# Cross-attention and a quantised FFN on one core: queries of batches 2 to 7 turned in 32-row blocks by SP and VectorE, mask terms and weight widening on ScalarE, and TensorE products that nobody reads

## The chip, the cores and the metric

One core of one Trainium2 chip runs the whole program in one launch. The metric is the device time of that launch in microseconds, the median of several runs. TensorE, VectorE (DVE), ScalarE (ACT), GpSimd (POOL) and SyncE (SP, which here only issues DMAs) run side by side and meet through semaphores. P = 128 is the number of partitions.

## What is computed

Eight batches of 512 rows of 512 numbers, cut to what matters:

```python
def xattn(v, k, q, mask, W, b):            # v = k = context, q = layernorm(x)
    scores = einsum('bqd,bkd->bqk', q, k) / sqrt(512)
    scores = where(mask, -1e9, scores)
    atted = einsum('bqk,bkd->bqd', softmax(scores), v)
    return einsum('bdl,ol->bdo', swapaxes(atted, -1, -2), W) + b
x = x + xattn(context, context, layernorm(x), mask, W_merge, b_merge)
y = fake_quant_activation(layernorm(x))    # one scale for the whole tensor, int8 grid
h = fake_quant_activation(silu(y @ q(w_gate).T) * (y @ q(w_up).T))
x = x + h @ q(w_down).T                    # q: each weight row on its own int8 grid; I = 1408
```

## The kernel before

**Two parts.** `attention()` does the first line for all batches and, beside it, brings the FFN weights on their grids; `ffn()` does the rest. Both write their five engine programs by hand: each engine executes its list in order, and every wait is a `wait_ge` on a semaphore. The order of the work is thus the order of the code of each engine.

**Precision.** In attention every float32 matrix is split in two float32r halves, `_hi` (a rounded copy, ScalarE) and `_lo` (the rest, VectorE or GpSimd), and a product is the sum hi x hi, hi x lo, lo x hi (`product`, lines 805 to 817): 12 matmuls of 128x512 for each 128-row tile, 48 for each of the three products of a batch. These are, on TensorE: `scores(n, k)` for tile k of batch n (lines 819 to 826), `merged(m, k)` for the batch before (m = n - 1, lines 828 to 833), and `mixed(n, k)` (lines 835 to 840), the product of probabilities and merge matrix. The loop is at lines 856 to 880. All three use the four PSUM banks `mm[k]`, so `scores(n + 1, k)` waits (`g_ready`) until `mixed_hi` (ScalarE, line 440) and `mixed_lo` (VectorE, line 632) have taken `mm[k]` of batch n, `merged` waits until the mask step has read the scores (`masked`), and `mixed` until the residual has been added (`x1_made`).

**The queries.** `norm1` (ScalarE, line 451) writes the normalised rows `qn`. TensorE turns them, `transposes(n + 1, T + k)` (line 789) ahead of `mixed(n, k)`: four 128x128 transposes into bank `tr[k]`. `transposed_hi` (ScalarE) and `transposed_lo` (VectorE, line 527) take them out as `qT_hi` and `qT_lo`.

**The context.** Its transposed form already avoids TensorE from batch 1 on: `load_cb` (SP, line 238) loads 32-row blocks of the context to the partitions where a transpose would put the block, in pieces of 32 numbers, and `turn_c` (VectorE, line 572) turns each 32x32 block in place. `turned_hi` (ScalarE) and `turned_lo` (GpSimd, line 377) split it.

**The rest of a batch.** VectorE: `mask_and_max` (line 583) adds the mask term `mneg`, takes the row maximum and, in a second step, `nmax`, its negative scaled; `invert_sum`, `probs_lo`; `row_stats1`; `row_bias1`; then for batch n - 1 `add_residual`, `row_stats2`, `row_min2`; then `weights_scale` (line 637), the largest of each row of a few weight tiles. ScalarE: `exps`, `probs_hi`, `norm1`, `context_hi`, `mixed_hi` and `weights_round` (line 467), which writes int8 `w8`. VectorE widens `w8` to float16 (`weights16`, line 666) at the start of the next batch, and SP turns it with DMA transposes (`turn_w`, line 262). GpSimd: `add_bias`, the powers of -1/2 (`make_rstd1`, `make_rstd2`), `make_mneg` (line 340, a whole batch in one step of 2,048 columns), `turned_lo`, `make_c_lo` (line 373). SP's order in a batch is at lines 299 to 322.

**Between the parts** each of the engines waits for all at the end of a block. The FFN's first steps find the largest value of the whole tensor with two small transposes on TensorE (lines 1252 to 1255), quantise batch 0, turn it (`turn`, line 1224) and start `gate_up`. After the last `gate_up` the scale of h is found, h is rounded (ScalarE) and widened (VectorE) in four pieces, and `down` (line 1264) begins.

## Time and profile before

| | before |
|---|---|
| median of 3 runs, us | 553.45 (553.35 to 553.67) |
| profiled execution: its time / its span, us | 553.71 / 551.9 |
| TensorE busy | 521.4 us, 94% |
| VectorE busy | 448.3 us, 81% |
| ScalarE busy | 284.7 us, 52% |
| GpSimd busy | 187.0 us, 34% |
| mean granted TensorE clock | 0.978 of full |
| attention part | 0 to about 302 us |

The span runs from the first to the last instruction; all other times are within it. A busy TensorE is not TensorE at its peak: a matmul's record (389 ns on average) is longer than the distance to the next (some 227 ns), so distances between starts tell more. Idle time of an engine is shown with what ended it.

### The profile page before, as it was taken

The numbers are of one execution on the slowest core, as the hardware profiler recorded it, in microseconds if no ns is written. First come the engines' busy times: TensorE is split into PE (matmuls) and PEld (weight loads), VectorE is DVE, ScalarE is ACT, GpSimd is POOL, SyncE is SP. The second block draws the span as 40 slices with busy tenths as digits, with TensorE's granted clock in tenths as the row PEclk, the third lists the DMA queues.
The fourth block names the chain that finished last, engine by engine and source line by source line (L and its number), as shares of the span: only waits on it lengthen the run. The fifth ranks groups of instructions, "written<-read, shape, count | busy, mean of one in ns | idle before, by whom it ended". The sixth has DMA issues, their size and how long they took to land. (4 is left out here: it accounts for less than half of the span.)

```text
span 551.9 us, 7208 instructions
## 1 busy us (share of the span) xinstructions
PE 521.4 (94%) x2386; PEld 341.1 (62%) x2386; DVE 448.3 (81%) x837; ACT 284.7 (52%) x417; POOL 187.0 (34%) x107
## 2 busy tenths in 40 slices
PE   5889899999999999999996799999999996999996
PEld 4768688888888888888884344444444442444442
DVE  5688999979997997898757487788778777698984
ACT  3755465644656564475241535554554533965610
POOL 3489766696663967685130000000000000000000
PEclk9989999999999999999998699999999999899999
DMA  9938759688497988943376428859301102679763
GB/s 262 213 115 139 162 169 171 182 160 217 159 184 163 165 254 181 143 158 111 110 62 185 179 78 290 218 166 297 99 16 38 38 1 97 266 293 396 262 230 152
DMA packets 120607, 93.60 MB, mean 170 GB/s; under 512 B 93440, under 2 KB 97536, under 8 KB 118016
## 3 DMA queue, kind: packets, MB, share of 16 engines
q1 hardware_dynamic: 120576, 93.21, 66.1%
q8 instruction: 16, 0.26, 0.2%
q14 instruction: 15, 0.12, 0.1%
HBM read 59.77 MB, written 25.43 MB: 154 GB/s over the span
## 5 line engine op out<-in xcount | busy, mean ns | idle before, releaser
L1248 PE MATMUL gu<-hid,gu_T 128*128 128x512 f16 x704 | 154.4, 383 | 0.8 <-DVE hid L1164 0.8
L1248 PEld LDWEIGHTS gu<-hid,gu_T 128*128 128x128 f16 x704 | 69.2, 99 | 85.7 <-issue 3.3
L1067 ACT ACTIVATE hid<-gu,gu_mul 128x512 f32<-128x512 f32 x88 | 59.6, 685 | 76.1 <-PE gu L1248 70.5
L1145 DVE SCALAR_TENSOR_TENSOR hid<-gu,gu_mul,hid 128x512 f32 (+1 forms) x88 | 65.1, 747 | 35.2 <-PE gu L1248 31.8
L1280 PE MATMUL gu<-wd_T,gu_T 128*128 128x512 f16 x264 | 60.4, 392 | 5.0 <-DVE gu_T L1189 5.0
L813 PE MATMUL mm<-wm_hi,p_hi 128*128 128x512 f32 x128 | 53.2, 416 | 3.7 <-DVE wm_lo L537 3.7
L1035 POOL PARTITION_ALL_REDUCE top<-hmax x1 | 0.4, 381 | 164.9 <-DVE hmax L1177 164.9
L1091 ACT ACTIVATE h<-hid,inv 128x512 int8<-128x512 f32 (+3 forms) x32 | 44.2, 1456 | 19.3 <-DVE gu_T L1189 15.4
L1153 DVE TENSOR_REDUCE hmax<-hid 128x1 f32 (+2 forms) x48 | 53.1, 1120 | 0.0
L813 PE MATMUL mm<-cT_hi,qT_hi 128*128 128x512 f32 x128 | 50.6, 395 | 1.7 <-DVE cT_lo L531 1.7
L815 PE MATMUL mm<-wm_hi,p_lo 128*128 128x512 f32 x128 | 50.9, 397 | 0.0
L814 PE MATMUL mm<-wm_lo,p_hi 128*128 128x512 f32 x128 | 50.5, 395 | 0.0
L1280 PEld LDWEIGHTS gu<-wd_T,gu_T 128*128 128x128 f16 x264 | 26.4, 100 | 38.5 <-DVE gu_T L1189 5.8
L815 PE MATMUL mm<-cT_hi,qT_lo 128*128 128x512 f32 x128 | 49.9, 390 | 0.0
L814 PE MATMUL mm<-cT_lo,qT_hi 128*128 128x512 f32 x128 | 49.8, 389 | 0.0
L815 PE MATMUL mm<-g_hi,c_lo 128*128 128x512 f32 x128 | 49.8, 389 | 0.0
L813 PE MATMUL mm<-g_hi,c_hi 128*128 128x512 f32 x128 | 49.8, 389 | 0.0
L814 PE MATMUL mm<-g_lo,c_hi 128*128 128x512 f32 x128 | 49.8, 389 | 0.0
L430 ACT ACTIVATE probs<-probs,nmax 128x512 f32<-128x512 f32 x32 | 23.2, 725 | 49.9 <-DVE nmax L593 49.6
L343 POOL TENSOR_SCALAR mneg<-mk 128x2048 bf16<-128x2048 uint8 x7 | 38.2, 5451 | 26.3 <-DMA mk<-in_mask_BxSxS_bk_dram 26.2
L444 ACT ACTIVATE g_hi<-mm 128x512 fp32r<-128x512 f32 x32 | 19.0, 597 | 44.9 <-PE mm L815 44.9
L375 POOL TENSOR_TENSOR c_lo<-cx,c_hi 128x2048 fp32r<-128x2048 f32 x8 | 36.9, 4618 | 14.9 <-ACT c_hi L465 14.8
(131 smaller groups left out, 934.3 us busy)
## 6 DMA issues: line engine op xcount, KB each, us to landing
h_dram<-hid SPq DMA_DIRECT2D x3, 2816.0 KB, 9.3
hid<-h_dram SPq DMA_DIRECT2D x3, 2816.0 KB, 11.9
cb<-in_ctx_dram SPq DMA_DIRECT2D x28, 256.0 KB, 6.6
cx<-in_ctx_dram SPq DMA_DIRECT2D x7, 1024.0 KB, 7.4
x<-in_x_dram SPq DMA_DIRECT2D x5, 1024.0 KB, 7.2
x_dram<-x SPq DMA_DIRECT2D x20, 256.0 KB, 3.5
xq<-x_dram SPq DMA_DIRECT2D x5, 1024.0 KB, 10.6
x<-x_dram SPq DMA_DIRECT2D x5, 1024.0 KB, 5.1
```

Of the source, the lines that this page charges most:

```text
L343: nc.gpsimd.tensor_scalar(mneg[:], mk[:], MASKED, None, ALU.mult).then_inc(mneg_made, 1)
L375: nc.gpsimd.tensor_tensor(c_lo[:], cx[:], c_hi[:].bitcast(F32), ALU.subtract).then_inc(c_ready, 1)
L430: nc.scalar.activation(probs[t % 3][:], probs[t % 3][:], ACT.Exp, bias=nmax[:, t:t + 1], scale=SCALE, accum_out=rsum[:, t:t + 1]).then_inc ...
L813: nc.tensor.matmul(bank[:], a_hi[:, t, cols], b_hi[:, t, :], start=t == 0, stop=False)
L814: nc.tensor.matmul(bank[:], a_hi[:, t, cols], b_lo[:, t, :], start=False, stop=False)
L815: last = nc.tensor.matmul(bank[:], a_lo[:, t, cols], b_hi[:, t, :], start=False, stop=t == T - 1)
L1067: nc.scalar.activation(silu[SILU_AT[i]], gu[2 * (i % 3)][:], ACT.Silu, scale=gu_mul[:, 0, i:i + 1]).then_inc(silu_done, 1)
L1091: nc.scalar.activation(h8[:, a:b, :].rearrange("p i l -> p (i l)"), hid[:, slot2(s), a * L:b * L], ACT.Copy, scale=inv[:, 1:2]).then_inc(h ...
L1145: nc.vector.scalar_tensor_tensor(hid[:, b % SLOTS, i * L:(i + 1) * L], gu[2 * (i % 3) + 1][:], gu_mul[:, 1, i:i + 1], silu[SILU_AT[i]], AL ...
L1153: nc.vector.tensor_reduce(hmax[:, k:k + 1], hid[:, b % SLOTS, lo * L:hi * L], AX_X, ALU.max, apply_absolute_value=True).then_inc(hmaxed, 1)
L1248: last = nc.tensor.matmul(gu[2 * (i % 3) + g][:], gu_T[:, g, h, i * P:(i + 1) * P], xT[p][:, h, :], start=h == 0, stop=h == T - 1)
L1280: last = nc.tensor.matmul(yb[T * (s % 2) + t][:], hq[s % 2][:, i, t * P:(t + 1) * P], wd_T[:, i, :], start=i == 0, stop=i == NI - 1)
```

## The change

1. **Queries of batches 2 to 7.** TensorE no longer turns them. SP moves each 32x128 block of `qn` to its turned place in a new buffer `qb` (`move_q`, 16 DMAs a batch), VectorE turns the 32x32 blocks in place (`turn_q`), ScalarE and GpSimd split them (`query_hi`, `query_lo`). To have pieces of 128 numbers rather than 32, the tables are kept in another order of columns (`blocks`, `columns`); the context blocks use the same order, so `load_cb` moves pieces of 128 numbers as well. Batch 1's `norm1` writes in that order and its queries are still turned by TensorE.
2. **Mask.** From batch 1 on ScalarE makes the mask terms (`make_mneg`, one step of 512 columns for each tile) into a buffer of two tiles; the tensor-wide step on GpSimd goes. `mask_and_max` gives `nmax` in one step; the step on one column goes. `probs` has two buffers in place of three.
3. **Weights.** The int8 values lie in the bytes of `wst` itself, and ScalarE widens them right after rounding (`weights16`), in place of VectorE at the start of the next batch.
4. **Orders.** ScalarE: `norm1` of the four tiles stands ahead of the last `probs_hi`; `query_hi` stands ahead of `mixed_hi`. VectorE: `row_bias1` one step earlier, `turn_q` between the residual rows and `weights_scale`. SP: `load_c` and `load_cb` earlier, `load_x` later. The load of `d_scale` moves from the end of `attention()` to the start of `ffn()`.
5. **Products nobody reads.** 15 at the end of `attention()`; in `ffn()` 2, 2, 11 and 4 around the small transposes and `turn`, and 20 before `down(0)`.

```diff
+                    def move_q(n):
+                        sp.wait_ge(q_ready, T * (n + 1))
+                        if n > 2:
+                            sp.wait_ge(qT_ready, T * (n - 2))
+                        for a in range(P // BLK):
+                            for k in range(P // BLK):
+                                sp.dma_start(qb[a * BLK:(a + 1) * BLK, :, k * P:(k + 1) * P],
+                                             qn[k * BLK:(k + 1) * BLK, :, a * P:(a + 1) * P]).then_inc(q_moved, 16)
...
                         if n:
+                            sp.wait_ge(c_ready, n)
+                            load_c(n)
                             sp.wait_ge(w_done, through(n - 1, w_turns))
                             load_w(n)
+                            if n < B - 1:
+                                move_q(n + 1)
                             for t in range(T):
                                 store_x1(n - 1, t)
...
+                    def query_lo(n):
+                        for t in range(T):
+                            gp.wait_ge(qT_hid, T * (n - 2) + t + 1)
+                            nc.gpsimd.tensor_tensor(columns(qT_lo, t), blocks(qb[:, t, :]), columns(qT_hi, t).bitcast(F32),
+                                                    ALU.subtract).then_inc(qT_ready, 1)
...
+                    def make_mneg(n, t):
+                        if t == 0:
+                            act.wait_ge(mask_in, 16 * (n + 1))
+                        act.wait_ge(masked, T * n + t - 1)
+                        nc.scalar.activation(mneg[:, t % 2, :], mk[:, t, :], ACT.Copy, scale=MASKED).then_inc(mneg_made, 1)
...
-                            elif t:
-                                probs_hi(n, t - 1)
+                            else:
+                                if t < 2:
+                                    make_mneg(n, t + 2)
+                                if t:
+                                    probs_hi(n, t - 1)
                         if not start:
+                            if not last:
+                                for t in range(T):
+                                    norm1(n + 1, t)
                             probs_hi(n, T - 1)
...
+                        if not (start or last):
+                            for t in range(T):
+                                query_hi(n + 1, t)
...
                         weights_round(n)
+                        weights16(n)
...
-                            out=probs[t % 3][:], in0=mm[t][:], in1=mneg[:, t, :], scale=1.0, scalar=LOWEST,
-                            op0=ALU.add, op1=ALU.max, accum_out=rmax[:, t:t + 1]).then_inc(masked, 1)
-                        dve.wait_ge(masked, T * n + t + 1)
-                        nc.vector.tensor_scalar(nmax[:, t:t + 1], rmax[:, t:t + 1], -SCALE, None,
-                                                ALU.mult).then_inc(nmaxed, 1)
+                            out=probs[t % 2][:], in0=mm[t][:], in1=mneg[:, t % 2, :], scale=-SCALE, scalar=-LOWEST,
+                            op0=ALU.add, op1=ALU.min, accum_out=nmax[:, t:t + 1]).then_inc(masked, 1)
...
+                            if not last:
+                                for t in range(T):
+                                    turn_q(n + 1, t)
                         weights_scale(n)
...
-                                if not last:
-                                    transposes(n + 1, T + k)
                                 mixed(n, k)
...
+                    for _ in range(15):
+                        nc.tensor.matmul(tr[0][:], c_hi[:, 0, 0:P], g_hi[:, 0, :], start=True, stop=True)
...
+                    keep_busy(2, gu[5])
                     pe.wait_ge(top_made, 1)
...
+                    keep_busy(2, gu[5])
                     pe.wait_ge(top_spread, 1)
...
+                    keep_busy(11, gu[5])
                     turn(0, 0)
+                    keep_busy(4, gu[5])
...
+                    keep_busy(20, tp[0])
                     for s in range(B):
                         down(s)
```

VectorE, end of an odd batch n, from the last residual row on (`cb`, `qb`: blocks to turn; `g_lo`: what scores(n + 1) waits for). Before:

```order
L615 BN_STATS st<-xq 128x6 [waits x1_made]
L618 TENSOR_REDUCE ln<-xq 128x1
L643 TENSOR_REDUCE gu_amax<-wst 128x2 [waits w_in]
L649 TENSOR_REDUCE d_amax<-wst 128x1
L653 TENSOR_SCALAR gu_scale<-gu_amax 128x2 [waits w_maxed]
L657 TENSOR_SCALAR d_step<-d_amax 128x1 [waits w_maxed]
L661 RECIPROCAL gu_inv<-gu_scale 128x2 [waits w_step]
L664 RECIPROCAL d_inv<-d_step 128x1 [waits w_step]
L531 TENSOR_TENSOR qT_lo<-tr,qT_hi 128x4x128 [waits t_hi]
L634 TENSOR_TENSOR g_lo<-mm,g_hi 128x512 [waits g_hid]
```

With the change:

```order
L681 TENSOR_REDUCE ln<-xq 128x1
L642 STREAM_TRANSPOSE qb<-qb 128x512 [waits q_moved]
L642 STREAM_TRANSPOSE qb<-qb 128x512 x3
L706 TENSOR_REDUCE gu_amax<-wst 128x2 [waits w_in]
L712 TENSOR_REDUCE d_amax<-wst 128x1
L716 TENSOR_SCALAR gu_scale<-gu_amax 128x2 [waits w_maxed]
L720 TENSOR_SCALAR d_step<-d_amax 128x1 [waits w_maxed]
L724 RECIPROCAL gu_inv<-gu_scale 128x2 [waits w_step]
L727 RECIPROCAL d_inv<-d_step 128x1 [waits w_step]
L697 TENSOR_TENSOR g_lo<-mm,g_hi 128x512 [waits g_hid] x4
```

The four block turns, behind a wait for the moves, stand ahead of the weights and of all `g_lo`; the `qT_lo` between them are gone.

ScalarE, an inner batch from the end of the weights to the last `p_hi`. Before:

```order
L479 ACTIVATE w<-wst,d_inv 128x1408
L430 ACTIVATE probs,rsum<-probs,nmax 128x512 [waits nmaxed] x2
L437 ACTIVATE p_hi<-probs,rinv 128x512 [waits g_done,rinved]
L430 ACTIVATE probs,rsum<-probs,nmax 128x512 [waits nmaxed]
L437 ACTIVATE p_hi<-probs,rinv 128x512 [waits rinved]
L430 ACTIVATE probs,rsum<-probs,nmax 128x512 [waits nmaxed]
L437 ACTIVATE p_hi<-probs,rinv 128x512 [waits rinved] x2
```

With the change (`wst<-wst` are the rounding of the down rows and the two widening steps):

```order
L519 ACTIVATE wst<-wst,d_inv 128x1408
L527 ACTIVATE wst<-wst 128x2x512 [waits w_rounded]
L533 ACTIVATE wst<-wst 128x1408
L466 ACTIVATE probs,rsum<-probs,nmax 128x512 [waits masked]
L456 ACTIVATE mneg<-mk 128x512 [waits masked]
L466 ACTIVATE probs,rsum<-probs,nmax 128x512 [waits masked]
L456 ACTIVATE mneg<-mk 128x512 [waits masked]
L473 ACTIVATE p_hi<-probs,rinv 128x512 [waits g_done,rinved]
...
L497 ACTIVATE qn<-xq,nmr,rstd 128x512 [waits q_moved,nmr1_made]
L497 ACTIVATE qn<-xq,nmr,rstd 128x512 [waits nmr1_made] x3
L473 ACTIVATE p_hi<-probs,rinv 128x512 [waits rinved]
```

Widening comes ahead of the first exponentials, two mask terms stand before the first `p_hi`, and the four `qn` before the last.

SP, in an even batch's loop from the weight loads on; before, then with the change:

```order
L255 DMA wst<-in_L_ffn_w_up_dram 128x2x512
L275 DMA x_dram<-xq 128x512 [waits x1_made] x4
L245 DMA xq<-in_x_dram 128x4x512 [waits x_free0,min2]
L241 DMA cb<-in_ctx_dram 32x64x32 [waits cT_ready]
L241 DMA cb<-in_ctx_dram 32x64x32 x3
L236 DMA cx<-in_ctx_dram 128x4x512 [waits c_ready]
```

```order
L280 DMA wst<-in_L_ffn_w_up_dram 128x2x512
L266 DMA qb<-qn 32x4x128 [waits qT_ready,q_ready]
L266 DMA qb<-qn 32x4x128 x15
L300 DMA x_dram<-xq 128x512 [waits x1_made] x4
L257 DMA cb<-in_ctx_dram 32x16x128 [waits cT_ready]
L257 DMA cb<-in_ctx_dram 32x16x128 x3
L270 DMA xq<-in_x_dram 128x4x512 [waits x_free0,min2]
```

Sixteen moves stand between the weight loads and the stores of x1; the context load has passed the load of x.

## Rows read from the trace of the kernel before

**Rows 1.** Timeline of TensorE: start, us, line, operation, tiles [idle before].

```profile
29.71 0.50 PE L813 MATMUL mm<-wm_hi,p_hi 128*128 128x512 f32 x1 [3.72 <-DVE wm_lo L537]
...
81.55 0.39 PE L813 MATMUL mm<-cT_hi,qT_hi 128*128 128x512 f32 x1
...
254.36 0.39 PE L813 MATMUL mm<-cT_hi,qT_hi 128*128 128x512 f32 x1
...
287.00 0.39 PE L813 MATMUL mm<-g_hi,c_hi 128*128 128x512 f32 x1
```

**Rows 2.** Timeline of VectorE: batches 0, 1 and 2, then batch 3.

```profile
26.83 1.62 DVE L602 SCALAR_TENSOR_TENSOR p_lo<-probs,rinv,p_hi 128x512 fp32r<-128x512 f32 x1
...
48.47 2.65 DVE L675 TENSOR_SCALAR expc<-expc 128x2 f32<-128x2 f32 x1 [1.05 <-ACT expc L522]
...
110.10 1.15 DVE L653 TENSOR_SCALAR gu_scale<-gu_amax 128x4 f32<-128x4 f32 x1
...
145.13 1.21 DVE L643 TENSOR_REDUCE gu_amax<-wst 128x2 f32<-128x1024 f32 x1
...
148.17 0.67 DVE L531 TENSOR_TENSOR qT_lo<-tr,qT_hi 128x512 fp32r<-128x512 f32 x1
...
156.32 0.69 DVE L589 CUSTOM_DVE_ANT_0 probs<-mm,mneg 128x512 f32<-128x512 f32 x1
...
158.71 1.02 DVE L602 SCALAR_TENSOR_TENSOR p_lo<-probs,rinv,p_hi 128x512 fp32r<-128x512 f32 x1 [0.17 <-ACT p_hi L437]
...
167.38 0.71 DVE L602 SCALAR_TENSOR_TENSOR p_lo<-probs,rinv,p_hi 128x512 fp32r<-128x512 f32 x1
...
179.28 2.29 DVE L643 TENSOR_REDUCE gu_amax<-wst 128x4 f32<-128x2048 f32 x1 [3.51 <-DMA wst<-in_L_ffn_w_up_dram]
...
181.97 0.66 DVE L531 TENSOR_TENSOR qT_lo<-tr,qT_hi 128x512 fp32r<-128x512 f32 x1
```

**Rows 3.** ScalarE: two groups of the page's kind, and its timeline in batch 3.

```profile
L465 ACT ACTIVATE c_hi<-cx 128x2048 fp32r<-128x2048 f32 x8 | 15.3, 1912 | 9.2 <-PE mm L815 9.1
L455 ACT ACTIVATE qn<-x,nmr,rstd 128x512 f32<-128x512 f32 x20 | 16.1, 803 | 2.3 <-DVE nmr L580 2.2
...
166.22 0.73 ACT L437 ACTIVATE p_hi<-probs,rinv 128x512 fp32r<-128x512 f32 x1 [0.90 <-DVE rinv L598]
```

**Rows 4.** Page, costliest groups: two of GpSimd (busy us, mean ns | idle before).

```profile
L380 POOL TENSOR_TENSOR cT_lo<-cb,cT_hi 128x512 fp32r<-128x512 f32 x28 | 35.9, 1311 | 1.0 <-ACT cT_hi L426 0.5
L375 POOL TENSOR_TENSOR c_lo<-cx,c_hi 128x2048 fp32r<-128x2048 f32 x8 | 36.9, 4618 | 14.9 <-ACT c_hi L465 14.8
```

**Rows 5.** SP: timeline, and the stores of x1 alone (issue ns, then landing).

```profile
1.18 1.84 SPq L287 DMA_DIRECT2D cx<-in_ctx_dram  x4
...
161.39 2.50 SPq L270 DMA_TRANSPOSE wd_T<-wst  x1
...
172.02 0.37 SPq L255 DMA_DIRECT2D wst<-in_L_ffn_w_gate_dram  x1
...
L275 SPq DMA_DIRECT2D x_dram<-x x20: 319/323/466, 102.1 to 298.8; - x20
...
DMA to landing us min/median/max: 2.3/2.9/6.8
```

**Rows 6.** Windows: us, TensorE busy (instructions), granted clock, DMA share, GB/s.

```profile
300.10:313.60 13.50, 7.17 (x29) 0.50 0.45 163
467.40:474.00 6.60, 5.54 (x14) 0.50 0.75 274
```

**Rows 7.** Timeline between the parts and before the down products.

```profile
302.31 0.37 PE L1253 MATMUL tp<-ident,tops 128*1 128x128 f32 x1 [4.26 <-DVE tops L1111]
...
309.13 3.17 PE L1248 MATMUL gu<-hid,gu_T 128*128 128x512 f16 x7 [0.79 <-DVE hid L1164]
...
468.46 17.21 PE L1280 MATMUL gu<-wd_T,gu_T 128*128 128x512 f16 x66 [4.96 <-DVE gu_T L1189]
...
472.80 1.49 DVE L1189 CAST gu_T<-h 128x2560 f16<-128x2560 int8 x1 [1.36 <-ACT h L1091]
```

More of the change, by code:

```diff
@@ L105, in attention @@
                 c_hi, c_lo = sb("c_hi", [P, T, D], F32R), sb("c_lo", [P, T, D], F32R)
-                probs = [sb(f"probs{i}", [P, L], F32) for i in range(3)]
+                probs = [sb(f"probs{i}", [P, L], F32) for i in range(2)]
                 p_hi, p_lo = sb("p_hi", [P, T, L], F32R), sb("p_lo", [P, T, L], F32R)
@@ L262, in turn_w @@
                     def turn_w(n):
-                        sp.wait_ge(w16, n + 1)
+                        sp.wait_ge(w16, through(n, parts))
                         for g in range(2):
@@ L436, in probs_hi @@
                             act.wait_ge(g_done, T * n)
-                        nc.scalar.activation(p_hi[:, t, :], probs[t % 3][:], ACT.Copy,
+                        nc.scalar.activation(p_hi[:, t, :], probs[t % 2][:], ACT.Copy,
                                              scale=rinv[:, t:t + 1]).then_inc(p_hid, 1)
@@ L575, in turn_c, with turn_q @@
                         nc.vector.transpose(cb[:, h, :], cb[:, h, :]).then_inc(cb_turned, 1)
+                    def turn_q(n, t):
+                        if t == 0:
+                            dve.wait_ge(q_moved, 256 * (n - 1))
+                        nc.vector.transpose(qb[:, t, :], qb[:, t, :]).then_inc(qb_turned, 1)
                     def row_bias1(n):
@@ L712, in _ @@
                         last, start = n == B - 1, n == 0
-                        if not start:
-                            weights16(n - 1)
                         for t in range(T):
@@ L757, in _ @@
                             else:
-                                if not last:
-                                    transposed_lo(n + 1, T + k)
                                 mixed_lo(n, k)
@@ L821, in scores @@
                             pe.wait_ge(g_ready, T * (n - 1) + k + 1)
[L822 removed]
+                        if n > 1:
+                            pe.wait_ge(qT_ready, T * (n - 2) + k + 1)
+                        else:
+                            pe.wait_ge(t_lo, turns(n, T + k) if n else max(turns(0, T + k), turns(0, T - 1)))
                         if n and k == 0:
@@ L871, in _ @@
                             else:
-                                if not last:
-                                    transposes(n + 1, T + k)
                                 mixed(n, k)
```

155 lines of the change are left out of this document (86 added, 69 removed).

## The prediction

> **What bounds the kernel now.** I read the page's busy shares first (TensorE far ahead of all others), then TensorE in order of time, then the other engines around one batch, then SP, then the clock. In the attention part batch 2 starts at 81.55 and batch 7 at 254.36, five periods of 34.56 us; batch 7, which turns no further queries, goes from 254.36 to 287.00, 32.64 us for the same 144 products [rows 1]. So the four groups of query transposes cost TensorE 1.92 us a batch, and a product 0.2267 us. Behind TensorE stands VectorE: in batch 3 (start 81.55 + 2 x 34.56 = 150.67) it goes from mask to p_lo to residual rows nearly without a pause and idles 3.5 us once, for weights [rows 2]. [...]
>
> **1. Transposes off TensorE (batches 2 to 7): a bound of 6 x 1.92 = 11.5 us.** It is had only if nobody else is later than 32.64 us, so I follow one batch n (2 to 6) from S, the start of its score products.
> - VectorE's mask for query tile 1 needs 24 products: S + 24 x 0.2267 + 0.2 = S + 5.65. ScalarE is not later: four roundings of about 0.65 and the new widening (2,048 columns; priced by c_hi, a copy of that width, 1.91 us [rows 3]; bounds 0 and twice that) follow the last g_hi and end near S + 4.5, and exps(0) needs 0.9.
> - In batch 3 p_lo(0) starts 158.71 - 156.32 = 2.39 after that mask [rows 2]. A mask term now stands between exps(1) and p_hi(0): a quarter of c_hi's 1.91, 0.5 (bounds 0.5 and the 0.80 of a qn). So S + 8.5, and 0.3 for GpSimd (below): S + 8.8.
> - In batch 3 p_lo(3) starts 167.38 - 158.71 = 8.67 after p_lo(0) [rows 2]. Now four qn, 0.80 us each and about 0.71 apart, stand ahead of p_hi(3) on ScalarE, which idled 0.90 there and ended 0.43 before p_lo(3) [rows 3]: 2.84 - 0.9 - 0.43 = 1.5 more, and - 0.1 for the removed nmax steps: 10.1. So p_lo(3) starts at S + 18.9 and ends at S + 19.6. Two in place of three probs buffers cost nothing either way, since VectorE's own order already holds it.
> - The residual rows of batch n-1 run from the end of p_lo(3), 168.0, to 179.28 - 3.51 = 175.8 [rows 2]: 7.7 us, S + 27.3. The 3.5 us of idle behind them was the cover for anything new there. turn_q, four transposes of 0.6 (the spacing of qT_lo and g_lo, 148.17 on): S + 29.7. They replace the four qT_lo of 0.6, but stand **ahead** of weights_scale and g_lo(0), where only one qT_lo stood.
> - weights_scale: even n 181.97 - 179.28 = 2.69, odd n 148.17 - 145.13 = 3.04 [rows 2]. GpSimd now runs qT_lo just then, 1.31 each as cT_lo, and c_lo behind them [rows 4]. In the trace gu_scale, a step on four columns, took 1.15 at 110.10 with cT_lo running, and p_lo 1.62 at 26.83 with the bias add [rows 2]. I add 0.6 (even, one such step) and 0.9 (odd, two), from bounds of 0 and 1.15 a step. Then g_lo(0) 0.65, on which scores(n+1, 0) waits.
> - **Period: 33.6 us (even), 34.2 (odd).** TensorE thus waits about 1 to 1.5 us a batch at the scores. Three even and two odd: 169.2 against 172.8, **-3.6 us**.
>
> [...]
>
> **2. SP and the move.** move_q waits for q_ready: the four qn end just before p_hi(3), at S + 18.2. SP is ready by then, barely: in an odd batch's wake its wd_T issue ends at 163.9 and the weight load behind it goes out at 172.0, 8.1 us later [rows 5]; from fp16 weights at S + 4.5, 5.1 us of turns, 8.1 and 0.8 of loads make S + 18.5; behind an even batch SP is free 6 us sooner. The 16 issues: 0.32 us each for stores of rows, 0.46 apart for loads [rows 5]; I take 0.37, as these too read SBUF: 5.9 us. Landing of the last: 2.3 to 6.8, median 2.9 [rows 5]. So q_moved is at S + 27.0 to 27.3, against S + 27.3 when turn_q wants it. **Cost 0, but with no slack**; bounds S + 25.6 (0.32 and 2.3) and S + 32.7 (0.46 and 6.8). The other queue changes (512 byte pieces for cb in place of 128, cx earlier, x later by one wait) free SP and I cost them at nothing: cb and x are wanted half a batch later.
>
> **3. Batches 0 and 1: +1.0 us.** Start-up: p_lo(2) took 1.62 at 26.83 beside the bias add and TensorE waited 3.72 us behind it until 29.71 [rows 1, 2]. The bias now lands earlier, since cb's small pieces stood ahead of it; gain 0 to 0.9, I take 0.6. Against it: expc, VectorE's first step before batch 1's masks, waits for ScalarE, which now has two mask terms (0.5 each) and the widening (1.9) ahead: 48.5 becomes 51.5 [rows 2]. VectorE no longer has the cast to do, and expc's 2.65 us shrink to the 1.3 of a GpSimd step, since c_lo is over by then: mask(1,0) at 53.2. From there as above: 4.2 to p_lo(0) (two masks' worth of ScalarE) and 0.3, then 10.1: p_lo(3) starts at 67.8 and ends at 68.5, residuals 76.2, turn_q 78.6, weights 3.9, g_lo 0.65: 83.1, less 0.6 = 82.5 for scores(2), before 81.55. Bounds -0.5 and +2.
>
> **4. Batch 7 and the last merged products:** no query work, TensorE bound as before: 0.
>
> **5. Products nobody reads.** Between the parts: 15 x 0.2267 = 3.4 us after the last merged product (297.9 to 301.4) end with VectorE's tail, behind which the next part's first small transpose comes at 302.31 [rows 7]; then 2, 2 and 11 of 0.2157 between the small transposes and 4 after turn. Each set fits the wait that it stands in, give or take 0.1. If the clock stays up, turn ends 0.4 earlier, and the 4.5 us from 309.13 to 313.6 at half clock [rows 6, 7] give back half, 2.25: **-2.65**. Bounds 0 and -2.8. Before the down products: 20 x 0.2157 = 4.3 us of the 5.0 idle. At full clock the 66 products from 468.46, 17.0 us to their last start, need 14.2 [rows 7], but the fourth piece of the first batch is cast only at 474.29: its 20 products end at 478.6, 22 more at 483.4, was 485.5: **-2.1**, bounds 0 and -2.8. (0.2157 is half the 0.43 spacing of the cold ones, with the small rest that warm ones show.)
>
> **Sum:** -3.6 + 1.0 - 2.65 - 2.1 = -7.35. On the span of 551.9 that is 544.5; the profiled execution took 553.71 and the median is 553.45, so 546.1. With the move in time and each term at its likelier bounds: 543 to 550.
>
> **Rivals.**
> - *The move is late (slower).* One mechanism: q_moved after S + 28.8. turn_q, weights_scale, g_lo and, on ScalarE, g_hi behind query_hi all stand behind it, and all of it repeats five times; break-even is 7.35 / 5 = 1.5 us late. With 0.46 us an issue and the median landing: S + 28.5, 1.2 late, 552; with a landing of 4.4 because load_w's megabyte is ahead on the same queue: 2.7 late, +13.5, about 560. For it: the tie above, and that wd_T's turn lands late in odd batches. Against it: stores of 0.32. [...] Chance past break-even 0.20, near it 0.04.
> - *TensorE bound all through.* VectorE's chain is 1 us shorter than I read and batches are 32.64: -9.6 in place of -3.6, so 540. For it: VectorE idles 3.5 us in the trace. Against it: the chain above, link by link. 0.10.
> - *GpSimd's lock at its worst (slower).* If c_lo gets in before gu_scale, gu_scale waits up to c_lo's 4.6 us [rows 4] in place of 0.6: with five batches at, say, half of that, 1.7 more each, 8.5 more: about 554.6. Against it: c_lo stands behind four qT_lo that begin only after turn_q's first piece, 5.2 us in all, and gu_scale comes 4.1 us after it. [...] 0.04.
> - *The extra products don't hold the clock,* since between them come small transposes and waits: then the forecast lacks up to 4.75 and gives up to 550.9. For: no row shows the clock after such a mix. Against: in both stretches of rows 6 it fell after TensorE had been idle. 0.10.
> - *Forecast* (move in time, VectorE's ring at 33.3 to 34.5): 0.52.
>
> **Numbers.** 546.1. About 0.1 lies under 540 and 0.1 over 558, which takes in half of the late move's prices. A measurement of this kernel can tell about 0.2%, 1.1 us. Faster: forecast 0.52, TensorE bound 0.10, most of the clock case 0.08: 0.70. Within 0.2%: the move near break-even 0.04 and the rest of the clock case 0.02: 0.06. Slower: late move 0.20, lock 0.04: 0.24.
>
> **What would show it.** Right: no transposes of qn after batch 1; batch starts 33.3 to 34.5 apart with TensorE waiting 0.5 to 2 us at its score products for g_lo, not for qT_lo; p_lo(3) 19 to 20 after S; turn_q right behind the last residual minimum; granted clock 1.0 from 300 to 314 and from 467 to 474. Wrong: VectorE waiting for the move (late), batches of 32.7 (TensorE bound), or clock 0.5 in those stretches.

## The result, and the profile after

The changed kernel takes **572.39 us** (median of 4, 569.78 to 574.31), the kernel before 553.56 beside it (553.35 to 555.66): ratio 1.033, 95% interval 1.029 to 1.036. The forecast was 546.1 and "faster". The profiled execution took 573.39 us, its span is 571.3; before 551.9.

TensorE in order of time, after: the first score product of batches 2 to 7, and the first merged product of batch 7 (the rows that answer to [rows 1]; L866 is the product of the two high parts).

```profile
84.04 0.80 PE L866 MATMUL mm<-cT_hi,qT_hi 128*128 128x512 f32 x1 [4.78 <-DVE g_lo L697]
122.65 0.50 PE L866 MATMUL mm<-cT_hi,qT_hi 128*128 128x512 f32 x1 [3.12 <-DVE g_lo L697]
160.78 0.50 PE L866 MATMUL mm<-cT_hi,qT_hi 128*128 128x512 f32 x1 [3.56 <-DVE g_lo L697]
199.50 0.80 PE L866 MATMUL mm<-cT_hi,qT_hi 128*128 128x512 f32 x1 [4.19 <-DVE g_lo L697]
239.22 0.50 PE L866 MATMUL mm<-cT_hi,qT_hi 128*128 128x512 f32 x1 [3.95 <-DVE g_lo L697]
277.13 0.69 PE L866 MATMUL mm<-cT_hi,qT_hi 128*128 128x512 f32 x1 [3.39 <-DVE g_lo L697]
...
311.49 0.39 PE L866 MATMUL mm<-g_hi,c_hi 128*128 128x512 f32 x1
```

The periods are 38.6, 38.1, 38.7, 39.7 and 37.9 us, where they were 34.56, and each batch now starts with 3.1 to 4.8 us in which TensorE waits for g_lo. The difference of the spans, 19.4 us, goes up in these rows: batch 2 starts 2.5 us later (84.04 against 81.55), five periods cost 20.3 more (193.1 against 172.8), batch 7 goes 34.4 us in place of 32.6 (1.7 more), and all that follows takes 571.3 - 311.5 = 259.8 in place of 551.9 - 287.0 = 264.9, 5.1 **less**.

Batch 3 of the changed kernel (start 122.65) on SP, then VectorE, then ScalarE; for SP the time is that of the issues.

```profile
134.94 0.72 SPq L285 DMA_DIRECT2D wst<-in_L_ffn_w_down_dram  x1
142.82 10.30 SPq L266 DMA_DIRECT2D qb<-qn  x16
153.17 2.06 SPq L300 DMA_DIRECT2D x_dram<-x  x4
155.28 2.59 SPq L257 DMA_DIRECT2D cb<-in_ctx_dram  x4
159.93 0.39 SPq L270 DMA_DIRECT2D x<-in_x_dram  x1
...
151.21 0.67 DVE L681 TENSOR_REDUCE ln<-x 128x1 f32<-128x512 f32 x1
154.63 2.49 DVE L642 STREAM_TRANSPOSE qb<-qb 128x512 f32<-128x512 f32 x4 [2.75 <-DMA qb<-qn]
157.04 1.18 DVE L706 TENSOR_REDUCE gu_amax<-wst 128x2 f32<-128x1024 f32 x1
158.14 1.60 DVE L712 TENSOR_REDUCE d_amax<-wst 128x1 f32<-128x1408 f32 x1
...
160.05 1.86 DVE L697 TENSOR_TENSOR g_lo<-mm,g_hi 128x512 fp32r<-128x512 f32 x3
...
155.38 2.41 ACT L462 ACTIVATE qT_hi<-qb 128x512 fp32r<-128x512 f32 x4 [7.03 <-DVE qb L642]
157.69 1.07 ACT L480 ACTIVATE g_hi<-mm 128x512 fp32r<-128x512 f32 x2
```

SP is ready at 135.7 and waits for the queries until 142.82. The 16 issues then take 10.3 us, 0.64 each (10.3 to 11.4 us in batches 2 to 6), and 1.5 us after the last one turn_q begins: at S + 32.0, with S the start of the batch's score products. VectorE had ended its residual rows at 151.9 and stood 2.75 us, and only then come turn_q, weights_scale and g_lo(0), on which TensorE waits. The view of DMA issues gives 2.0 us from issue to landing (median). In the six batches whose moves these are (1 to 6) VectorE waits 18.6 us in all for the move; TensorE waits 23.0 us for g_lo ahead of the scores of batches 2 to 7.

The granted clock in stretches (columns: stretch, its length, then busy time and count of instructions of PE, PEld, DVE, ACT and POOL, then clock, DMA share and GB/s): the score stages of batches 2 and 5, the stage behind that of 5, the score stage of 7, and two stretches behind the last merged product, for those at 0.50 in [rows 6].

```profile
84.00:97.60 13.60, 13.56 (x48) 11.05 (x49) 9.93 (x21) 9.08 (x16) 10.87 (x7) 0.80 0.99 141
199.50:213.40 13.90, 13.89 (x49) 11.22 (x50) 9.95 (x21) 8.64 (x16) 10.92 (x7) 0.78 0.74 174
213.40:234.20 20.80, 20.80 (x93) 17.22 (x92) 15.07 (x36) 9.78 (x15) 6.57 (x5) 1.00 0.55 177
277.10:289.70 12.60, 12.57 (x48) 10.27 (x49) 8.58 (x17) 7.81 (x14) 10.96 (x7) 0.86 0.32 61
...
311.50:334.00 22.50, 21.41 (x107) 14.85 (x106) 15.32 (x50) 7.41 (x9) 2.02 (x2) 1.00 0.74 191
485.00:500.00 15.00, 14.00 (x64) 5.79 (x63) 9.08 (x15) 11.29 (x9) 1.20 (x2) 1.00 0.71 264
```

Two things are to be seen. The unread products do what they were to do: both stretches are at 1.00, and so is all from 311.5 to the end. And each stall at the scores brings what they take away elsewhere: the 48 score products, 10.9 us at full clock (48 x 0.2267), last 12.6 us in four batches and 13.6 and 13.9 in two, since a part of them runs at half clock. In batch 2 the granted clock reads 0.50 from 84.0 to 88.8 and the products start 0.43 us apart; from 89.6 on it reads 1.00 and they start 0.23 apart.

### The profile page after: what moved, and what is told of

Same layout as the page of the kernel before. It is cut to its first block and busy times, and to the rows that moved or that the text cites. A ratio compares the mean times of both kernels' runs of the same rounds, so it can differ in the third digit from the quotient of the medians.

```text
span 571.3 us, 7224 instructions
## 1 busy us (share of the span) xinstructions
PE 531.0 (93%) x2344; PEld 345.1 (60%) x2344; DVE 436.0 (76%) x797; ACT 314.8 (55%) x456; POOL 171.1 (30%) x124
## 5 line engine op out<-in xcount | busy, mean ns | idle before, releaser
L1310 PE MATMUL gu<-hid,gu_T 128*128 128x512 f16 x704 | 152.1, 379 | 0.0
L866 PE MATMUL mm<-cT_hi,qT_hi 128*128 128x512 f32 x128 | 56.6, 442 | 24.7 <-DVE g_lo L697 23.0
L1351 PE MATMUL gu<-wd_T,gu_T 128*128 128x512 f16 x264 | 58.0, 379 | 1.0 <-DVE gu_T L1251 0.9
L867 PE MATMUL mm<-cT_lo,qT_hi 128*128 128x512 f32 x128 | 55.0, 430 | 0.0
L868 PE MATMUL mm<-cT_hi,qT_lo 128*128 128x512 f32 x128 | 55.0, 429 | 0.0
L866 PE MATMUL mm<-wm_hi,p_hi 128*128 128x512 f32 x128 | 50.8, 397 | 4.1 <-DVE wm_lo L599 3.3
L866 PE MATMUL mm<-g_hi,c_hi 128*128 128x512 f32 x128 | 49.8, 389 | 0.0
L866 PEld LDWEIGHTS mm<-cT_hi,qT_hi 128*128 128x128 f32 x128 | 27.2, 213 | 33.3 <-DVE g_lo L697 25.5
L400 POOL TENSOR_TENSOR cT_lo<-cb,cT_hi 128x512 fp32r<-128x512 f32 x28 | 35.8, 1308 | 33.3 <-ACT cT_hi L450 33.2
L406 POOL TENSOR_TENSOR qT_lo<-qb,qT_hi 128x512 fp32r<-128x512 f32 x24 | 29.8, 1275 | 43.9 <-ACT qT_hi L462 43.9
```

Source lines behind the costliest of these rows:

```text
L400: nc.gpsimd.tensor_tensor(columns(cT_lo, t), blocks(cb[:, t, :]), columns(cT_hi, t).bitcast(F32), ALU.subtract).then_inc(cT_ready, 1)
L406: nc.gpsimd.tensor_tensor(columns(qT_lo, t), blocks(qb[:, t, :]), columns(qT_hi, t).bitcast(F32), ALU.subtract).then_inc(qT_ready, 1)
L866: nc.tensor.matmul(bank[:], a_hi[:, t, cols], b_hi[:, t, :], start=t == 0, stop=False)
L867: nc.tensor.matmul(bank[:], a_hi[:, t, cols], b_lo[:, t, :], start=False, stop=False)
L868: last = nc.tensor.matmul(bank[:], a_lo[:, t, cols], b_hi[:, t, :], start=False, stop=t == T - 1)
L1310: last = nc.tensor.matmul(gu[2 * (i % 3) + g][:], gu_T[:, g, h, i * P:(i + 1) * P], xT[p][:, h, :], start=h == 0, stop=h == T - 1)
```

## The experiments

Four theories stood at the start. Theory 1: SP's time for 16 issues makes the move late. Theory 2: what moved to ScalarE makes VectorE's chain late without it. Theory 3: the order of the work behind the landing multiplies the delay. Theory 4: the half clock after each stall does. Every kernel was timed beside the kernel before on its chip.

**Unread products alone.** The kernel before with the 15, 2, 2, 11, 4 and 20 products, and nothing else of the change.

> The kernel before with nothing added but the products that nobody reads: 15 behind the last merged product, 2, 2, 11 and 4 around the small transposes of the second part, 20 ahead of the down products. Theory (they keep the clock, and the changed kernel's rest of the program is 5.1 us shorter, 259.8 against 264.9, because of them): 548.4 +-0.7, granted clock 1.0 from 300 to 314 and from 467 to 474. Rival (the 5.1 us come from the scale load that moved, or from the other state in which the first part ends): 552 to 554, with the clock still at 0.50 in one of the two stretches.

550.86 us (548.07 to 551.94) against 554.23, ratio 0.993 (0.990 to 0.996): outside both ranges. Its profiled execution takes 549.8 - 290.0 = 259.8 us from the last merged product on, to a tenth what the changed kernel takes, at clock 1.00. But its first two batches were 3.0 us longer than before's (scores(2) at 84.53), with part of batches 0 and 1 at half clock (0.92 granted from 0 to 84.5, against 0.98 to 81.55 before). The start-up varies between executions (scores(2) at 81.55 and 84.53 in two kernels that are alike up to there). So the theory holds for the 5.1 us by the trace and the clock (1.00 from 300 to 314 and from 467 to 474); the time, 3.4 us less, would not have shown it by itself.

**Four moves in place of sixteen.**

```diff
-                        for a in range(P // BLK):
-                            for k in range(P // BLK):
-                                sp.dma_start(qb[a * BLK:(a + 1) * BLK, :, k * P:(k + 1) * P],
-                                             qn[k * BLK:(k + 1) * BLK, :, a * P:(a + 1) * P]).then_inc(q_moved, 16)
+                        for k in range(P // BLK):
+                            sp.dma_start(qb[:, :, k * P:(k + 1) * P],
+                                         qn[:, :, k * P:(k + 1) * P]).then_inc(q_moved, 16)
```

> The changed kernel, with 4 moves of 128 partitions in place of 16 of 32: the same bytes in the same pieces of 512 bytes, but no block changes its partitions, so the queries of batches 2 to 7 are turned wrongly. Theory 1 (SP's issue of each move, 0.65 us, makes the move late): the move starts at S + 20.2 as before and is in at S + 25.5 to 26.5; VectorE finds it done when its residual rows end; turn_q comes 2.7 us sooner and the half clock at the scores goes in most batches: 549 to 559. Rival (the bytes or the pieces set it: 64 KB pieces through the 16 engines or the weight load ahead of them): turn_q still at S + 31 or later, 569 to 573. If an issue of four times as many pieces takes four times as long, it is the rival too.

**545.22 us** (544.66 to 546.26), ratio 0.984 (0.980 to 0.988), for a kernel that leaves out the change of partitions and so computes other queries. Batch 4 (start 147.90 on TensorE, then SP, then VectorE):

```profile
147.90 0.50 PE L865 MATMUL mm<-cT_hi,qT_hi 128*128 128x512 f32 x1 [1.18 <-DVE g_lo L696]
...
166.80 2.74 SPq L265 DMA_DIRECT2D qb<-qn  x4
...
175.78 2.48 DVE L641 STREAM_TRANSPOSE qb<-qb 128x512 f32<-128x512 f32 x4
```

The move starts at S + 18.9, its four issues take 2.7 us, and turn_q follows the residual rows with no idle time, at S + 27.9. Periods are 33.99 to 34.12, the wait at the scores is 1.0 to 1.9 us, and the clock stays at 1.00. One issue of 512 pieces costs 0.68 us, one of 128 pieces 0.64: here it is the number of issues that costs, not bytes or pieces. Theory 1 holds, and the rival falls. The time lies under the expected 549 to 559: with the score stage at full clock the move itself starts at S + 18.9, not at S + 20.1 to 20.7 as in the changed kernel.

**weights_scale ahead of turn_q**, with g_hi(0) ahead of query_hi.

```diff
-                            if not last:
-                                for t in range(T):
-                                    turn_q(n + 1, t)
                         weights_scale(n)
+                        if not (start or last):
+                            for t in range(T):
+                                turn_q(n + 1, t)
```

> The changed kernel, with weights_scale ahead of turn_q on VectorE, and g_hi(0) ahead of the rounding of the moved queries on ScalarE. The move stays as late as it is. Theory 3 (the order behind the late move costs as much as the move: VectorE idles 2.75 us and then does the 2.7 to 3.0 us of weights_scale while TensorE waits for g_lo): VectorE's idle time for the move falls under 0.5 us a batch, scores(n+1,0) start 2.0 to 2.7 us sooner, and where the stall falls under about 2 us the half clock goes too: six times 2.5 and some of six times 1.7: 547 to 558. Rival (scores then wait for qT_lo as long as they did for g_lo, since both hang on the landing): 568 to 573, with TensorE's wait named qT_lo.

564.91 us, ratio 1.019 (1.014 to 1.024): between the theories. VectorE's idle time for the move is nearly gone (0 to 0.9 us), the stall at the scores is down to 1.7 to 2.8 and the clock stays up (1.00 from 80 to 300); but periods are 36.8 to 38.0. VectorE and GpSimd in batch 3 of this kernel (start 118.98), and TensorE in batch 2:

```profile
122.56 4.38 DVE L695 TENSOR_SCALAR ve<-ln 128x4 f32<-128x4 f32 x1
122.30 4.61 POOL L395 TENSOR_TENSOR c_lo<-cx,c_hi 128x2048 fp32r<-128x2048 f32 x1
...
105.78 0.50 PE L868 MATMUL mm<-wm_hi,p_hi 128*128 128x512 f32 x1 [1.95 <-DVE ln L674]
```

A step on four columns takes 4.38 us while c_lo runs on GpSimd, and ends with it, at 126.9; a like step on other numbers, ve<-mv, takes 0.17 us at 136.81 in the changed kernel. The step ve<-ln takes 2.8 us there (2.86 at 124.71, to 127.57, with c_lo to 127.55), hidden while VectorE waits for the scores anyway. Here it pushes masks and p_lo back, TensorE waits a second time, ahead of mixed, and the move itself starts only at S + 22. The kernel before has the same in expc, 2.65 us to 51.12, with c_lo to 51.09. So the kernel is 7.5 us faster than the changed one, but two things changed at once: the order, and with the shorter stalls the clock. What the order alone is worth isn't shown: at full clock the old order has periods of 36.9 (next run), and this one has none clearly shorter. The rest of the late move moved along the ring.

**A bridge ahead of the scores.**

```diff
+                        for _ in range(14 if n > 1 else 0):
+                            nc.tensor.matmul(tr[1][:], wm_hi[:, 0, 0:P], wm_hi[:, 0, :], start=True, stop=True)
                         for k in range(T):
                             scores(n, k)
```

> The changed kernel, with 14 products that nobody reads (3.0 us) ahead of scores(n,0) of batches 2 to 7, where TensorE stands 3.1 to 4.8 us. [...] Rival (the chain behind the move does not start from the score products, so that a faster score stage only waits longer later): periods still 38 to 39, 570 to 573, though the clock is 1.0.

570.50 us (568.60 to 572.51), ratio 1.030 (1.026 to 1.035). The time is in the rival's range, and its interval overlaps the changed kernel's: theory 4 falls as an account of the whole loss. (By my estimate from the score stages of the changed kernel, full clock would give back 4 x 1.7 + 2.7 + 3.0 = 12.5 us, a time of about 560.) In single batches it holds. The bridge kept the clock in batches 2, 4, 5 and 6 (1.00 in their score stages); in 3 and 7 the score stage still lasts 12.65 us, at 0.87. In batches 4 and 5, where nothing else came in, the periods are 36.94 and 36.92, in place of the changed kernel's 38.7 and 39.7: the late move at full clock. Batch 5, on TensorE, SP and VectorE:

```profile
197.45 0.50 PE L866 MATMUL mm<-cT_hi,qT_hi 128*128 128x512 f32 x1 [0.79 <-DVE g_lo L697]
...
216.44 10.30 SPq L266 DMA_DIRECT2D qb<-qn  x16
...
228.19 2.49 DVE L642 STREAM_TRANSPOSE qb<-qb 128x512 f32<-128x512 f32 x4 [2.70 <-DMA qb<-qn]
```

turn_q starts at S + 30.7 in place of 27.9 with four moves, and the period is 36.92 in place of 34.0: 2.9 us a batch for the lateness. The rest up to the changed kernel's mean of 38.6, 1.7, I put down to the half clock. The start of the move agrees: it is at S + 18.9 to 19.0 in batches 4 to 6 here, and at S + 20.1 to 20.7 in all batches of the changed kernel. But the 1.7 rests on two batches, and the whole run didn't gain it. In batch 6, at full clock too, the move landed later (turn_q at S + 31.8), and the period is 37.9 in both kernels. In batch 2 the faster chain ran into something else that waits on SP behind the 16 issues: the rows x of the next batch.

```profile
91.25 1.29 DVE L625 BATCH_NORM_STATS2 st<-xq 128x6 f32<-128x512 f32 x2 [2.44 <-DMA xq<-in_x_dram]
```

**Queries on TensorE again**, all else as changed: move_q, turn_q, query_hi and query_lo go, and the steps of the kernel before take their place:

```diff
                             else:
+                                if not last:
+                                    transposes(n + 1, T + k)
                                 mixed(n, k)
```

> The changed kernel with one part undone: the queries of batches 2 to 7 are turned by TensorE again, rounded from its banks by ScalarE and subtracted by VectorE, as before. The mask terms, the widening, the order of the loads, the two probs buffers and the unread products stay as changed. Theory (only the move costs; the rest of the change is worth its 5 us behind the attention part and nothing in it): TensorE bound again at 34.5 to 34.6 a batch, 547 to 550. Rival (what moved to ScalarE, mask terms between exps and p_hi, four qn ahead of p_hi(3), makes VectorE's chain late by itself): periods over 35 and 552 or more.

548.46 us (548.04 to 548.86), ratio 0.988 (0.984 to 0.992); periods 34.55 to 34.57, TensorE without idle time from 81.08 to the end of the attention part. Theory 2 falls: mask terms, widening and the four qn ahead of p_hi(3) cost nothing while TensorE is the bound. The whole loss comes with the moved queries.

**Two queues for the move.** SP issues 10 moves; ScalarE the other 6, behind p_hi(3):

```diff
+                        for i in range(10, 16):
+                            a, k = divmod(i, P // BLK)
+                            nc.scalar.dma_start(qb[a * BLK:(a + 1) * BLK, :, k * P:(k + 1) * P],
+                                                qn[k * BLK:(k + 1) * BLK, :, a * P:(a + 1) * P]).then_inc(q_moved, 16)
```

> The changed kernel, with the 16 moves split: 10 issued by SP, 6 by ScalarE behind p_hi(3), where ScalarE has 7 us idle. All bytes and pieces as changed. Theory 1 (the issues of one queue, 0.65 us each, are the cost): the SP share takes 6.5 us, the move is in at S + 28 against VectorE's S + 27.9, and periods are 34.0 to 34.6 as with four moves: 545 to 550. Rival (the 16 moves of 32 partitions take their time in the DMA engines, whoever issues them): turn_q at S + 31 or later and 565 or more. Second rival (an issue costs ScalarE more than SP, over 1 us each, and its roundings of cT and c come late): 552 to 560, TensorE waiting for cT_lo or c_lo.

548.45 us (546.16 to 551.87), ratio 0.990 (0.986 to 0.994); periods 34.02, 34.12, 34.58, 34.17, 34.02. Batch 3 (start 115.36), SP and ScalarE:

```profile
134.33 7.05 SPq L266 DMA_DIRECT2D qb<-qn  x10
...
134.33 4.17 ACTq L464 DMA_DIRECT2D qb<-qn  x6
138.61 2.19 ACT L450 ACTIVATE cT_hi<-cb 128x512 fp32r<-128x512 f32 x4 [3.69 <-issue]
```

Sixteen moves with the same bytes, in time but for 0.5 us in batch 4, and nearly the periods of four moves: the DMA engines are not the limit here. An issue costs ScalarE 0.70 us, which delays its cT_hi by 3.7 us and lengthens no period; the second rival falls. This sharpens theory 1 to the issue time of one queue. That time is the larger part of the move: 10.3 us of issues on one queue against 2.0 of landing, 7.05 against 2.2 on two.

**g_lo(0) between turn_q and weights_scale**, the move still late.

```diff
+                        if not start:
+                            mixed_lo(n, 0)
                         weights_scale(n)
```

> The changed kernel, the move as late as it is, with g_lo(0) between turn_q and weights_scale on VectorE and g_hi(0) ahead of the rounding of the queries on ScalarE. With weights_scale first, VectorE's idle time was filled, but g_lo stayed behind both. Theory 3 (what stands between the landing and g_lo matters): scores(n+1,0) at landing + 2.5 + 0.65, or at qT_lo(0), landing + 2.6, so 2.7 to 3 us sooner in each batch than as changed, stall under 1.5, no half clock: 550 to 557. Rival (TensorE then waits as long for qT_lo, or the 2.8 us of ve, locked by c_lo, move into the chain as they did with weights_scale first): 561 to 568.

564.18 us, ratio 1.016 (1.012 to 1.020); periods 36.9 to 37.7: the rival's range. scores(n,0) came sooner (stall 1.7 to 2.5), but the score stage then lasts 12.5 us at full clock (1.00 from 118.6 to 131.1), since g_lo(1) stands behind weights_scale. The rival's second part is seen too: ve, 2.2 us long (in batch 3 to 126.54, with c_lo to 126.51), now stands at S + 5.7, ahead of the masks.

**The last two edits together, and ve ahead of turn_q.** To the two above comes:

```diff
+                            for k in range(T):
+                                aggregate2(n - 1, k)
+                            variances2(n - 1)
                             if not last:
                                 for t in range(T):
                                     turn_q(n + 1, t)
```

> The attempt to beat both kernels: two queues for the move, g_hi(0) ahead of the rounding of the queries on ScalarE, g_lo(0) ahead of weights_scale on VectorE, and the row aggregates with ve ahead of turn_q, where c_lo of GpSimd is not running (it took 2.8 to 4.4 us behind g_lo). With the move in at S + 28, turn_q to S + 31 (ve's 0.6 included) and g_lo(0) at S + 31.6, before TensorE's own 32.64: TensorE bound, periods 32.7 to 33.2, scores(2) at 78 to 80: 537 to 541. Rival (the move is still the last, by 1 us or more): 542 to 547. If the second rival of the two queues holds: over 548.

550.14 us (546.58 to 552.06), ratio 0.989 (0.985 to 0.993): a miss of both ranges, and the ground given for a time over 548, a dear issue on ScalarE, isn't what came. scores(n,0) waits for nothing, ve takes 0.4 to 1.3 us in its new place, but periods are 34.1 to 36.1. Batch 3 of this kernel on TensorE shows the cause, the same as in the run before: the first product of scores(n,1), 4.2 us behind scores(n,0):

```profile
120.81 0.50 PE L880 MATMUL mm<-cT_hi,qT_hi 128*128 128x512 f32 x1 [1.20 <-DVE g_lo L710]
```

**g_lo(0) and g_lo(1) ahead of weights_scale**, and g_hi(0) and g_hi(1) ahead of query_hi; two queues and early ve stay.

```diff
                         if not start:
                             mixed_lo(n, 0)
+                            mixed_lo(n, 1)
                         weights_scale(n)
```

> Two queues as before, ve ahead of turn_q, and now g_lo(0) and g_lo(1) (and g_hi(0), g_hi(1) on ScalarE) ahead of weights_scale and of the rounding of the queries. In the last attempt scores(n,0) waited for nothing, but the score stage lasted 12.5 us in place of 10.9: g_lo(1) stood behind weights_scale, 3 us, and TensorE wants it 2.7 us after g_lo(0). Theory: g_lo(0) at S + 31.5, g_lo(1) at S + 32.1, weights_scale to S + 35.3, g_lo(2) at S + 36 against a need of 32.64 + 5.4 = 38: TensorE bound, score stage 10.9 us, periods 32.7 to 33.2: 538 to 543 (start-up moves this by 1.5 either way). Rival (VectorE's work behind g_lo, pushed past the start of the scores, makes mask(1) and then p_lo(3) late, and TensorE waits ahead of mixed as in the last attempt): periods 34 to 35, 546 to 550.

**546.39 us** (544.62 to 549.42), ratio 0.985 (0.981 to 0.988). Score stages last 10.9 to 11.0 us and one period is the bare 32.64, but the others are 34.3 to 36.5: in four batches TensorE waits ahead of mixed, as in batches 2 and 5 here (the record of 0.61 in the first row is one at half clock: 0.53 granted from 103.5 to 107):

```profile
103.50 0.61 PE L882 MATMUL mm<-wm_hi,p_hi 128*128 128x512 f32 x1 [1.84 <-DVE ln L686]
...
207.98 0.50 PE L882 MATMUL mm<-wm_hi,p_hi 128*128 128x512 f32 x1 [2.98 <-DVE ln L686]
```

weights_scale now ends behind the start of the scores, ScalarE's rounding and widening behind it, and exps(0) behind those. The rival's mechanism and its range, with single periods up to 1.5 us longer than it had.

**Pieces of 2 KB.** norm1 writes qn in another layout, so that each move takes one run of 512 elements from a partition:

```diff
-                                sp.dma_start(qb[a * BLK:(a + 1) * BLK, :, k * P:(k + 1) * P],
-                                             qn[k * BLK:(k + 1) * BLK, :, a * P:(a + 1) * P]).then_inc(q_moved, 16)
+                                sp.dma_start(qb[a * BLK:(a + 1) * BLK, k, :],
+                                             qn[k * BLK:(k + 1) * BLK, a, :]).then_inc(q_moved, 16)
```

> The changed kernel, 16 moves of 32 partitions on SP as changed, with another layout of qn and qb, in which each move takes one piece of 2 KB from a partition in place of four of 512 bytes. The output is the reference's. Four moves of 512 pieces each took 0.68 us of issue, 16 of 128 pieces 0.65: theory A (an issue has a fixed price for SBUF to SBUF, whatever the pieces): still 0.6 to 0.65 each, 568 to 573. Theory B (the price is that of a pattern of three dimensions against one of two, as in the x1 stores of 128 pieces of 2 KB, 0.32): 16 issues in 5.2 to 6 us, the move in at S + 27.5, periods 34.0 to 34.3: 545 to 549.

571.25 us, ratio 1.031 (1.028 to 1.034). Theory A:

```profile
141.25 10.06 SPq L270 DMA_DIRECT2D qb<-qn  x16
```

0.63 us each with a quarter of the pieces. Theory B falls: the plain pattern is no cheaper. One batch, 4, kept the clock at its scores (1.00 from 158.9 to 169.9) behind a stall of 2.60 us: its move starts at S + 18.9 and its period is 37.3, where the others are 37.6 to 39.0; the move of batch 3 above starts at S + 20.6.

**All of it**: the pieces of 2 KB in the version with two g first, whose two queues then read `qn[k * BLK:(k + 1) * BLK, a, :]` too.

> The two above together: pieces of 2 KB, two queues, two g first, ve ahead of turn_q. If theory B holds, the move is in at S + 24 and nothing hangs on it: 537 to 541. If theory A holds, the same as without the pieces of 2 KB, within 1.5 us.

547.34 us (545.41 to 550.59), ratio 0.989 (0.984 to 0.993): as theory A had it, within a microsecond of the version without the 2 KB pieces.

**The widening later**, in the version with two g first.

```diff
                                 if t:
                                     probs_hi(n, t - 1)
+                                if t == 1:
+                                    weights16(n - 1)
...
-                        weights16(n)
+                        if last:
+                            weights16(n)
```

> The version with two queues, ve early and two g first, and in addition the widening of the weights (1.9 or 2.4 us of ScalarE) moved behind p_hi(0) of the next batch. There TensorE waited 1.4 to 3.0 us ahead of mixed in four of the six batches, because exps(0) stood behind rounding and widening, which now start only when weights_scale is done at S + 2 to 3. Theory: p_lo(0) comes 1.5 to 1.9 us sooner, TensorE's waits ahead of mixed fall under 1 us, periods 32.64 to 33.8: 540 to 544. Rival (SP turns the weights 4 us later, so that the weight load and with it the move, behind it on SP, start after S + 20): turn_q waits for the move again, 546 to 552.

552.35 us (547.88 to 557.95, 12 runs), ratio 0.995 (0.993 to 0.998): the rival, and more. TensorE's waits ahead of mixed fell to 0.2 us in three batches, with 1.4 in one, but SP turns the weights 4 us later, and all behind it on SP is late: turn_q waits again (0.5 to 2.2 us), and VectorE for x (up to 3.4), here in batches 5 and 6. And the stall at the scores is back (1.7 to 2.2 us in four batches); in two of them, 2 and 6, the clock fell with it, to 0.87 in the stage, which lasts 12.6 us. The last row is the first product of batch 6:

```profile
217.60 2.49 DVE L659 STREAM_TRANSPOSE qb<-qb 128x512 f32<-128x512 f32 x4 [2.17 <-DMA qb<-qn]
...
232.26 1.29 DVE L642 BATCH_NORM_STATS2 st<-x 128x6 f32<-128x512 f32 x2 [3.38 <-DMA x<-in_x_dram]
...
220.72 0.49 PE L885 MATMUL mm<-cT_hi,qT_hi 128*128 128x512 f32 x1 [2.22 <-DVE g_lo L714]
```

The best version that computes the right output is the one with two g first, 546.39 us. Its interval and those of the two queues alone and of the queries on TensorE overlap, so it beats both kernels, but not clearly its neighbours.

## Why the prediction was wrong, point by point

- **Part 2, SP and the move: the step that failed.** "I take 0.37, as these too read SBUF: 5.9 us ... Cost 0, but with no slack." An issue from SBUF to SBUF costs 0.64 us, twice a store's 0.32 and above the 0.46 of loads that I had taken for the upper bound [rows 5]: 10.3 us. (With this one number the forecast's own sum has the move 4.1 us late and the time at 566.6.) The other two parts of that sum: q_ready was forecast at S + 18.2 and is 18.9 to 19.0 at full clock (20.1 to 20.7 in the changed kernel, whose score stages run at half clock in part), and a landing of 2.9 is 2.0. So turn_q can start at S + 30.7 at full clock and started at 31.8 to 33.6 as it ran, where 27.0 to 27.3 was forecast. Even the outer bound, 32.7, which took a landing of 6.8, was passed in batch 5; the chance of 0.20 for "late" rested on 0.46 as the dearest issue.
- **The rival of the late move was the right one, and too cheap.** 2.7 us late was priced at 13.5 us, about 560. Measured at full clock, 2.9 us a batch (36.9 against 34.0) would have given about that. What was missing is the **half clock**: no term asked what a stall of 3 to 5 us at the scores does to TensorE's clock, though [rows 6, 7] show it for stalls of 4.3 and 5.0 us. It costs 1.7 us in the scores of four batches, 2.7 and 3.0 in two, and the links that start from them are late: the move starts 1.2 to 1.8 us later. By the bridge's two undisturbed batches that is 1.7 more a period.
- **Against the forecast span** of 544.5 the changed kernel is 26.8 us longer: five periods 193.1 against 169.2, 23.9; scores(2) at 84.04 against 82.5, 1.5; batch 7 34.4 against 32.64, 1.7, all of it half clock; the rest of the program 0.35 less than forecast.
- **Part 1, the periods with the move in time: right.** Forecast 33.6 and 34.2, measured 33.99 to 34.12 with four moves. Forecast p_lo(0) at S + 8.8, p_lo(3) at 18.9, residual rows to 27.3; measured 8.75, 19.5 and 27.9. The 0.6 that the chain is late is made good by weights_scale, which was forecast too dear, so that the sum is in part luck. With four moves the whole kernel takes 545.2 against the 546.1 forecast; here too errors cancel, for its batch 2 starts 2.7 us sooner than forecast (79.8 against 82.5) and its periods sum to 170.2 against 169.2. What the rows call batch 3, with its start at 150.67, is batch 4 (81.55 + 34.56 is batch 3); the lengths of the links are those of batch 4, and no sum changes.
- **Part 3, batches 0 and 1: wrong for batch 1.** +1.0 forecast. Batch 1 took 36.9 us before (38.5 with the unread products alone, part of it at half clock), 38.8 in the changed kernel, where it holds a late move, and 35.9 with four moves and with two queues: with the move in time it is 1.0 shorter, where the forecast had it 1.6 longer. With four moves the first mask of batch 1 comes at 51.4 and not at 53.2; expc takes 0.33 us there, not 1.3. Batch 0 is unsettled: its length varies by more than its 0.6 between profiles that are alike up to there.
- **Part 4, batch 7:** 0 forecast, 1.7 measured, half clock; 32.8 with four moves.
- **Part 5, unread products: right.** -4.75 forecast, -5.1 measured: from merged(7) to the down products 178.5 in place of 181.5, 3.0 (forecast 2.65), and from there to the end 81.35 in place of 83.4, 2.1, as forecast.
- **GpSimd's lock on gu_scale**, a VectorE step that lasts longer while GpSimd runs, stayed small in the changed kernel: weights_scale took 2.96 us (even) and 3.01 (odd) against 3.3 and 3.9 forecast, and the rival of the lock at its worst did not come. The long lock sits two steps later, on ve, 2.8 us and hidden there in the changed kernel; it came out once the order was changed (4.38 with weights_scale first).
- **TensorE bound all through, 540:** it would have needed g_lo 1.4 us sooner. Each edit that brought it sooner put another part of the ring behind.

## What to carry to other kernels

Count a transfer's issues as work of the engine that makes them: here the 16 moves between partitions cost 16 x 0.64 = 10.3 us, and that time, not bytes or the 2.0 us of landing, decided when the last one was in. Take the price from issues that stand back to back, of the same kind (a store took 0.32 us alone, 0.52 back to back, a move 0.64). Where a link has no slack, price the loss to the end: everything behind it in the order of its engine, the loads behind it on its queue, and the clock of TensorE behind the stall, which fell to half here after each of 12 stalls of 3.06 to 4.78 us. And in a ring of engines that are all nearly full, a step that is moved out of one wait turns up in the next; look at what then waits before counting the gain.

## What the runs showed that was not expected

- The price of an issue from SBUF to SBUF hardly depends on its pieces: 0.64 us for 32 partitions and 128 pieces of 512 bytes, 0.63 for 32 pieces of 2 KB, 0.68 for 128 partitions and 512 pieces. ScalarE pays 0.70. A megabyte of x costs 0.39. Why, no run here shows.
- The 0.32 us of a store [rows 5] was the price of one that stands alone. Before, each store waited for its rows; in the changed kernel the four of a batch are ready and follow the moves back to back, 2.06 us for four (the row at 153.17 above), with a median of 0.45 over 20 of them:

```profile
L300 SPq DMA_DIRECT2D x_dram<-x x20: 319/450/588, 115.2 to 323.3; - x20
```

- From batch 2 on to the end of the attention part, every stall of TensorE of 3.06 us or more, 12 in three kernels (six in the changed kernel, one with the bridge, five with the pieces of 2 KB), was followed by products at half clock, 0.43 us apart in place of 0.23. Most shorter ones were not, up to 2.83 us at the scores (weights_scale first) and 2.98 ahead of mixed (two g first). But six shorter ones were: 1.79 at the scores behind 14 unread products (the bridge, batch 7), 2.09 and 2.22 at the scores with the widening later, and ahead of mixed 1.84 with two g first and 1.85 and 2.87 with all of it. So the length of the stall alone doesn't decide, and what does stays open.
- GpSimd's subtractions on the new, strided pattern cost what they cost before: 1.27 us a piece, against 1.31 in [rows 4].
